# Reordering the weight preparation between the two passes of an adaLN block with gated linear attention

## The reference, cut to what matters

```python
mod = (silu(c) @ wmod).reshape(1, 6, 1, -1)          # c is 1 x 512, wmod 512 x 3072
sa, ca, ga, sb, cb, gb = (mod[:, n] for n in range(6))
ga = (2 * (ga >= 0) - 1) * max(abs(ga), 0.25)        # the same for gb
h = layernorm(x) * (1 + ca) + sa                     # x is 8192 x 512
# attention: q, k, v, gate, decay from h; recurrence over the tokens, 16 heads of 64
out = rmsnorm(gla_scan(q, k * gate, v, decay)) * norm_w
out = out * sigmoid(h @ Wog.T)                       # output gate, Wog is 1024 x 512
x = x + ga * (out @ Wo.T)                            # Wo is 512 x 1024
h = layernorm(x) * (1 + cb) + sb
x = x + gb * ffn(h, W_r, W_k, W_v, mu_r, mu_k)       # three 512 x 512 products
```

## Time and profile before

| | us |
|---|---|
| median of 3 runs | 3674.97 (3674.07 to 3676.39) |
| profiled execution | 3674.58 |
| its span | 3672.8 |
| last work of the attention pass ends | 2280.7 |
| first stage load issued | 2283.0 |
| last remainder of the second `prepare` ends | 2329.35 |
| first matmul of the output pass | 2335.1 |

### The profile page before, as it was taken

How to read it: one execution, slowest core, us unless ns; L and a number is a source line. 1 busy time by engine, 2 the same in 40 slices (tenths; PEclk the granted TensorE clock), 3 DMA queues, 4 the chain that set the end, 5 groups by cost and what they waited for, 6 DMA issues and landing times. The chain is left out here.

```text
span 3672.8 us, 73725 instructions
## 1 busy us (share of the span) xinstructions
PE 3596.5 (98%) x25349; PEld 3339.3 (91%) x25349; DVE 2145.5 (58%) x5207; ACT 1546.0 (42%) x3904; POOL 464.7 (13%) x883
## 2 busy tenths in 40 slices
PE   7999999999999999999999997899999999999998
PEld 7999999999999999999999997688888888888887
DVE  4555555555555555555555556566566655666566
ACT  4445445445545445445445453333332323233332
POOL 0111111111111111111111111100000000000000
PEclk8999999999999999999999999899999999999999
DMA  4222322322322322322232223412221122212220
GB/s 156 76 60 65 81 60 58 87 62 56 87 63 55 86 64 54 81 71 54 75 77 54 75 71 87 162 69 71 77 91 69 69 80 85 75 69 74 75 91 23
DMA packets 206044, 274.89 MB, mean 75 GB/s; under 512 B 13968, under 2 KB 146080, under 8 KB 206000
## 3 DMA queue, kind: packets, MB, share of 16 engines
q1 hardware_dynamic: 206000, 274.31, 25.6%
HBM read 189.84 MB, written 84.41 MB: 75 GB/s over the span
## 5 line engine op out<-in xcount | busy, mean ns | idle before, releaser
L813 POOL TENSOR_TENSOR k_lo<-kg,k_hi 128x256 fp32r<-128x256 f32 x256 | 186.7, 729 | 1501.1 <-ACT q_hi L588 1501.1
L609 ACT ACTIVATE decay<-cum_rows,w_cur 128x128 f32<-128x128 f32 x1024 | 327.8, 391 | 20.6 <-POOL cum_rows L807 12.7
L55 PE MATMUL psJ<-h_hi,w_g_hi 128*128 128x256 f32 x1024 | 314.7, 307 | 8.3 <-DVE h_lo L675 4.6
L577 ACT COPY q<-psJ 128x256 f32<-128x256 f32 x256 | 95.5, 373 | 501.1 <-PE psJ L57 501.1
L55 PE MATMUL psJ<-h_hi,w_q_hi 128*128 128x256 f32 x1024 | 304.4, 297 | 0.0
L683 DVE SCALAR_TENSOR_TENSOR kg<-gate,psJ 128x256 f32<-128x256 f32 x256 | 107.8, 421 | 333.0 <-PE psJ L57 305.5
L56 PE MATMUL psJ<-h_lo,w_q_hi 128*128 128x256 f32 x1024 | 286.2, 279 | 0.0
L57 PE MATMUL psJ<-h_hi,w_k_lo 128*128 128x256 f32 x1024 | 286.1, 279 | 0.0
L56 PE MATMUL psJ<-h_lo,w_g_hi 128*128 128x256 f32 x1024 | 285.9, 279 | 0.0
L57 PE MATMUL psJ<-h_hi,w_q_lo 128*128 128x256 f32 x1024 | 285.8, 279 | 0.0
L55 PE MATMUL psJ<-h_hi,w_k_hi 128*128 128x256 f32 x1024 | 285.6, 279 | 0.0
(11 more groups left out here) (226 smaller groups left out, 10601.8 us busy)
## 6 DMA issues: line engine op xcount, KB each, us to landing
cum_rows<-cum_dram SPq DMA_DIRECT2D x256, 256.0 KB, 5.4
o_rows_dram<-o SPq DMA_DIRECT2D x256, 128.0 KB, 1.8
o_rows<-o_rows_dram SPq DMA_DIRECT2D x32, 1024.0 KB, 5.4
an_norm_x<-in_L_attn_x_dram SPq DMA_DIRECT2D x32, 512.0 KB, 3.9
h_dram<-h_hi SPq DMA_DIRECT2D x32, 512.0 KB, 2.7
h_dram<-h_lo SPq DMA_DIRECT2D x32, 512.0 KB, 3.8
h_hi<-h_dram SPq DMA_DIRECT2D x32, 512.0 KB, 3.7
h_lo<-h_dram SPq DMA_DIRECT2D x32, 512.0 KB, 4.6
```

What stands on the lines that cost most here:

```text
L55: nc.tensor.matmul(out, w_hi, x_hi, start=first, stop=False)
L577: nc.scalar.copy(q[:, b, :], psJ[USES.index(("q", b)) % 2][:, 0:T]).then_inc(s["by_act"], 1)
L609: last = nc.scalar.activation(decay[:, 2 * c + h, :], cum_rows[:, p % 4, 2 * c + h, :], ACT.Exp, bias=w_cur[:, 3, c, 2 * p + h:2 * p + h + ...
L813: nc.gpsimd.tensor_tensor(k_lo[:, :], kg[:, p, :], k_hi[:, :].bitcast(F32), ALU.subtract).then_inc(s["k_lo"], 1)
```

## The change

Both halves of the output gate's weight now come first, then GA and GB, then both halves of the output weight. The jobs from SB on stay where they were. Nothing else is touched.

```diff
-            jobs = [mod[GA], mod[GB], og[0], o[0], og[1], o[1], mod[SB], mod[CB],
+            jobs = [og[0], og[1], mod[GA], mod[GB], o[0], o[1], mod[SB], mod[CB],
                     (rows(w_v, 0), t["gb"], cols["v2"]), (rows(w_r, 0), None, cols["r"]), (rows(w_k, 0), None, cols["k2"])]
             prepare(nc, t, jobs, "s")
```

## The result

The changed kernel took 3683.03 us (median of 11 runs, 3680.83 to 3684.69) against 3674.73 us of the kernel before (11 runs in the same comparison): ratio 1.0021, 95% interval 1.0012 to 1.0030. The forecast was 3682.6, in a range of 3679.0 to 3684.6, with more than 0.2% slower as the likelier side (0.53). Its profiled execution took 3681.31 us with a span of 3679.6. In all comparisons of this document two executions, one of e1 (11836.62 us) and one of the kernel before (10486.13 us), count as slow and are in no ratio.

The account below looks back on a forecast made before the run. The prediction took a chain over the engines between the two passes, not the loads, to set that stage's end; +8.3 us there and -0.5 at the output pass's start gave +7.8, so 3682.6 us, range 3679.0 to 3684.6.

Parts of the forecast that it names:

- tail to the last remainder: Stage between the passes, from the end of CB's sums to the last remainder: 11.8 us, same order and clock as before.
- The order of one engine is the path: Stage between the passes: VectorE works in order, so GA and GB start after og[1] and gb is written at 2304.9, before 2297.17.
- The cover of the second scaling goes: Between o[0] and o[1]: og[1] no longer covers GpSimd's scaling of o[1], 2.8 us, with some 3 us of idle TensorE.
- Half clock in both short bursts: TensorE turns o[0] and o[1] at half clock after pauses: 16 transposes in 3.65 us, at full clock 1.97.
- Rival (A): Clock stays high over the pauses between o[0] and o[1]: +4.9 us, 3679.7 us; chance 0.15.
- (B): Early og transposes raise the clock and it holds to the output pass: -0.6 us, 3674.1 us; chance 0.05.
- GpSimd and VectorE beside each other: SB's and CB's sums partly overlap GpSimd's scaling of w_v: 6.2 us, within bounds of 5.6 and 6.95.
- w_k's load stays covered: Stage between the passes: w_k's load, issued at about 2325.2, lands at 2330.5, about 3 us before TensorE needs it.
- Rival (C): w_k's load becomes the last ready, taking 10 us instead of 5.3: +9.4 us, 3684.2 us; chance 0.08.
- The start of the output pass, -0.5: TensorE's cold start averages 4.5 to 5 us instead of 5.7 at half clock; half the difference is won, -0.5 us.

Follow-up runs that it names:

- e1: Changed kernel with GA and GB put back in front of og[0] and og[1], o[0] and o[1] still adjacent: 3677.04 us, ratio to the kernel before 1.0004.
- e2: Changed kernel with the order og[0], GA, GB, o[0], og[1], o[1] at the start: 3679.12 us, ratio to the kernel before 1.0007.
- e3: Changed kernel with two buffers for scaled weights instead of one: 3678.16 us, ratio to the kernel before 1.0007.
- e5: Changed kernel with five stage buffers instead of four: 3682.83 us, ratio to the kernel before 1.0022.
- e8: e7 plus 25 unread transposes on TensorE at the start of the output pass: 3671.15 us, ratio to the kernel before 0.9990.
- e4: Changed kernel with unread filler transposes of the identity in TensorE's pauses: 3679.24 us, ratio to the kernel before 1.0008.
- e6: Kernel before with w_r ahead of w_v and SB and CB moved to the end: 3671.34 us, ratio to the kernel before 0.9991.
- e7: e6 with two scaled buffers and five stage buffers: 3672.19 us, ratio to the kernel before 0.9992.

## Why the prediction was right

The chain that was walked on the old trace, against the new one:

| step | predicted us | measured us |
|---|---|---|
| first issue to the first transpose of `og[0]` | 5.7 | 5.55 |
| `og[0]` and `og[1]`, up to GA's sums | 7.7 | 7.77 |
| sums of GA and GB | 5.6 | 5.60 |
| to `gb` written | 2.9 | 2.92 |
| `o[0]` scaled | 2.8 | 2.80 |
| `o[0]` turned, to the next scaling | 3.8 | 3.65 |
| `o[1]` scaled | 2.8 | 2.75 |
| `o[1]`, to its last remainder | 5.35 | 5.14 |
| sums of SB and CB | 6.2 | 6.14 |
| tail to the last remainder | 11.8 | 11.68 |
| stage | 54.65 | 54.00 |
| against before (46.36) | +8.3 | +7.64 |

- *The order of one engine is the path.* Right: VectorE reached GA 7.8 us after the first transpose, and e1 shows that putting GA and GB back wins 5.6 of the 7.6 us, 4.4 of them by the earlier gates.
- *The cover of the second scaling goes.* Right: 2.92 us of pause in the changed kernel and in e1, 0.30 in e2, none in e3.
- *Half clock in both short bursts.* Right in the main: 3.42 and 3.63 us. The first was a little shorter, since the clock rose before its end, as it did in `og[1]` at the start of the stage. It was at 1.00 from 2310 to 2313 and had fallen again when `o[1]` came, so the second burst was at half clock after a rise and a fall in the pause, which the prediction did not have. Rival (A) needed 2 us for both and is out; (B) needed a clock that held over the pauses and is out.
- *GpSimd and VectorE beside each other.* The middle value of 6.2 was right (6.14 from the last remainder of `o[1]`, 6.23 from the start of the sums). GpSimd's scaling of w_v took 3.99 us before, 3.39 in the changed kernel and 2.70 in e3, where it ended 0.2 us after the sums began; the two sums took 6.95, 6.23 and 5.60 us. The Trainium skill ("SBUF — State Buffer", section "Who interferes with whom") has a VectorE instruction with two inputs in SBUF contend with a GpSimd instruction that reads SBUF, and calls the pair of ports that they share an exclusive lock; its words on blocking for the whole instruction stand with VectorE's 2-port modes, and the prediction carried them over. The rows agree that the two contend and that it goes with the overlap. They don't show one strictly after the other: in the 3.99 us of the scaling before, 2.70 us of GpSimd's work and about 2.6 us of VectorE's (5.60 less the 2.42 before it and the 0.54 behind it, an estimate) went through.
- *w_k's load stays covered.* Right: issued at 2323.67, which is 2324.5 on the prediction's time axis (predicted 2325.2), and e5 takes it away altogether without effect. Rival (C) is out.
- *The start of the output pass, -0.5.* This term was mis-sized. It gave 0.05 us (19.31 against 19.36 from load to load): from the first product on 0.15, for a half-clock stretch 0.3 us shorter, of which a wait for h_lo 0.1 us longer took the most back. The share of one half was right, and so was the mean start: in the nine executions profiled without the warm start the stretch was some 3.3 to 5.7 us long, 4.8 on average (an estimate, from where the products go from 0.63 to 0.40 us). The changed kernel's happened to be a long one. And the gain stands against the one profiled execution before, with its 5.7 us; the median before has average starts in it already, so between medians the term should be near nothing. e8 shows that even without such a stretch the next limit is near: ScalarE's table load and sigmoid.

That the forecast, 3682.6, came so close to the median of 3683.03 is partly luck: a stage estimated 0.65 too long made up for a gain at the start of the output pass that didn't come, and medians of 11 runs are uncertain by more than that: the interval of the ratio is 3.3 us wide to each side, and the medians differ by 8.3 us where the stage differs by 7.64. One sum of the prediction is off by a little: three fifths of 0.72 and all of 0.08 are 0.51, not 0.53.

## What to carry to other kernels

An order of jobs that all engines share is a chain through the engine that has the most to do (here VectorE), so work put ahead of a vector that another engine waits for delays it by that engine's time for it, however idle the others are. Between two jobs that go through the same single buffer, keep one that does not; it hides the preparation (TensorE's pause before `o[1]` was 2.92 us without it and 0.30 with it). To forecast such a reordering, walk the chain with durations of the old trace, and carry both clock rows for a burst that comes behind a pause: the same code had it at 1.97 and at 3.68 us.

## What the runs showed of the hardware

- The granted clock was at 0.50 while TensorE worked on GA and GB in the changed kernel (2300 to 2309), with matmuls of one column and pauses between them. In e4, where it had been kept up until then (0.94 from 2296 to 2302), it was at 0.50 from 2303 on, and the 26 dense fillers that followed ran at half clock for most of their 4.93 us. Whether the kind of matmul or the pauses let it fall, no run tells apart.
- The clock was out of step with the work: 1.00 from 2310 to 2313 in the changed kernel, when TensorE did almost nothing, and 0.50 from 2314 to 2316, in the middle of the next burst.
- The same work doesn't always get the same clock. The kernel before, e6, e7 and e8 have the same first jobs, and `o[0]` is turned 17.4 to 17.5 us after the first issue in all four; the 16 transposes took 1.97, 2.46, 1.97 and 3.68 us.
- Stretches of nothing but transposes ran at full clock (e4, 2309 to 2320 at 1.00), and the 25 of e8 left the clock up for the first product.
- A half-clock start of 5.7 us at the head of the output pass cost 1.1 us more than one of 3.3 us and 1.2 more than none, as ScalarE's chain was next.
